# A rank-128 correction's third pass, issued as 32-row products in four banks side by side

## The chip, the cores and the metric

The kernel runs on one core of one Trainium2 chip. The metric is the device time of one execution in microseconds (us), lower being better; three runs of the kernel before are given, and one further execution was profiled.

## What is computed

The input x holds 16 batches of 512 tokens by 1024 features. A conditioning stage forms `(n*v + sum(v)) * relu(cond @ W3 + b3)`, multiplies it by `W2` (1024x1024), adds a bias and applies relu. Its result y goes through a feed-forward stage:

```
base_out   = y @ W_base + b_base                      # 1024 x 1024
shared_out = (y @ A_s) @ B_s                          # rank 16
gates      = softmax(y @ W_router + b_router), top 2 of 6 experts
routed_out = sum over e of ((y @ A_r[e]) * w_e) @ B_r[e]     # rank 16 each
out        = x + base_out + shared_out + routed_out
```

The low-rank paths of the experts and the shared one are laid side by side into one correction of rank 6 + 7*16 = 118, padded to 128 rows: `low` (128 x 1024, the B matrices) times `h` (128 x 512 tokens, gated). All products are kept accurate to about fp32 by splitting each operand into a rounded part `hi` (fp32r) and a rest `lo`, and adding three passes: hi*hi, hi*lo and lo*hi.

## The kernel before, in words

Batches are taken in pairs, eight pairs. The two large products, by `W2` (groups g = 0 to 7) and by `W_base` (g = 8 to 15, the W_base stage), are done with a seven-product scheme for 2x2 block matrices: per pair there are products n = 0 to 6, each of a 512x512 weight block by a 512x512 activation block. A product has four tiles j = 0 to 3 (128 output features each, one PSUM bank of 512 tokens each) and four steps k (128 rows of the contraction each); each step has the three passes of `three()` at L1608 to L1613. So a tile is 12 matmuls. Products 2, 3, 4 and 6 add onto a bank that already holds an earlier product (`ONTO`).

In the W_base stage the low-rank correction is added behind the twelve matmuls of each tile of products 4, 5 and 6, as three more passes over 128 rows: `low_hi` by `hi`, `low_hi` by `lo`, `low_lo` by `hi`. That makes 15 matmuls for a tile. For product 6 the operands are `ha_hi` and `ha_lo`. Product 2 is followed by four correction products of its own (`low_rank_c11`), which the change leaves alone.

The order on every engine is written out by hand and tied by semaphores. The ones that matter here:

- `bank_done` counts finished tiles on TensorE (PE), one for each tile, in program order. The VectorE (DVE) eviction `c21` of tile j of product 6 (L1142, called from `c21`) waits for its count; PE waits for `c21_done` before product 0 of the next pair overwrites the bank (`bank_free`).
- `c22_done` counts the DVE evictions of product 5; tile j of product 6 waits for the one of its bank.
- `lr_lo_done` tells that `ha_lo` (made by `lr_low_d` on DVE) is ready.
- On DVE, between the evictions of product 6, stand the operands of the next pair: the order is `low(g+1,0,0)`, `t1`, then for j = 1 to 3 `low(g+1,0,j)`, `c21(g,j-1)`, `t1(g+1,j)`. `low` (L1085) makes the `lo` part of step j of the next pair's product 0, and PE waits for it (`lo_done`) at step k of tile 0.
- The store queue (SP) writes each evicted tile to `outT` in the order of `c21_done`; at the very end the last tile is evicted and stored in two halves (L1604, L574, L1034).

Near the start `turn()` issues, between ordinary matmuls of 128 rows, four transposes of 16 rows each (L1628), of which the trace has two such groups.

Of the kernel before, what the change touches and what calls it, by code (L numbers as in the profile page):

```python
# [11 lines left out]
P = 128  # L12
# [15 lines left out]
H = 4  # L28
# [8 lines left out]

def adaln_ffn(nc, xT, condT, w3, w2, b2, wbase, bbase, acat, bcat, brouter, outT, E, R):
    NB, K, _, T = xT.shape
    NP = NB // 2  # L40
    D = K * P
# [15 lines left out]
    with ExitStack() as ctx:  # L57
        def sb(name, shape, dt=F32, stack=ctx):
            return stack.enter_context(nc.sbuf_tensor(name, shape, dt))

        def sem(name):
            return ctx.enter_context(nc.semaphore(name))
# [90 lines left out]
        low_hi = sb("low_hi", [AC, D], F32R)  # L153
        low_lo = sb("low_lo", [AC, D], F32R)
        ha_hi = sb("ha_hi", [AC, T], F32R)
# [6 lines left out]
        ps = ctx.enter_context(nc.psum_tensor("ps", [P, 8, T], F32))  # L162
# [46 lines left out]
        bank_done = sem("bank_done")  # L209
# [46 lines left out]
        lr_lo_done = sem("lr_lo_done")  # L256
        lr_done = sem("lr_done")
        c11_low = sem("c11_low")
        c11_out = sem("c11_out")
        x12_loaded = [sem(f"x12_loaded{j}") for j in range(H)]  # L260
        x22_added = sem("x22_added")
# [5 lines left out]
        def slot(g, n, k):  # L267
            return H * ((g + n) % 2) + k

        def op_no(g, n, k):  # L270
            return OPS * g + H * n + k + 1
# [8 lines left out]
        def four(g, j):  # L280
            return H * g + j + 1
# [1326 lines left out]
        def _(pe):  # L1608
            def three(out, wh, wl, a_h, a_l, start, stop, onto=False):

                nc.tensor.matmul(out, wh, a_h, start=start, stop=False, skip_group_check=onto)  # L1611
                nc.tensor.matmul(out, wh, a_l, start=False, stop=False, skip_group_check=onto)  # L1612
                return nc.tensor.matmul(out, wl, a_h, start=False, stop=stop, skip_group_check=onto)  # L1613
# [32 lines left out]
            def bank_free(g, n, j):  # L1646
                if n == 0:
                    if g > 0:
                        pe.wait_ge(c21_done, four(g - 1, j))
                elif n == 1:  # L1650
                    if g == 0:
                        pe.wait_ge(q_ready, 2)
                    elif j >= 2:
                        pe.wait_ge(c11_done, four(g, j - 2))
                    elif g == 1:
                        pe.wait_ge(c11_done, H)
                    elif g <= NP:
                        pe.wait_ge(c11_done, four(g - 1, j + 2))
                    else:
                        pe.wait_ge(c11_low, four(g - NP - 1, j + 2))  # L1660
                elif n == 2:
                    pe.wait_ge(p0_copied, four(g, j))
                elif n == 3:
                    pe.wait_ge(u2_copied, four(g, j))
                elif n == 4:
                    pe.wait_ge(u4_copied, four(g, j))
                elif n == 5:
                    pe.wait_ge(c12_done, four(g, j))
                else:
                    pe.wait_ge(c22_done, four(g, j))  # L1670

            def group(g, n, j, low_rank=None):
                bank_free(g, n, j)
                bank = j if n != 1 else Z_BANK + j % 2
                cols = slice(j * P, (j + 1) * P)
                for k in range(H):
                    if j == 0:
                        pe.wait_ge(lo_done, op_no(g, n, k))
                        if g == 0:
                            pe.wait_ge(w2_lo_done, H * n + k + 1)  # L1680
                        elif g == NP:
                            pe.wait_ge(wb_lo_done, wb_no(n, k))
                    s = slot(g, n, k)
                    mm = three(ps[:, bank, :], w_hi[:, n, k, cols], w_lo[:, n, k, cols], act_hi[:, s, :],
                               act_lo[:, s, :], k == 0 and n not in ONTO, k == H - 1 and low_rank is None, n in ONTO)
                    if j == H - 1 and k < H - 1:
                        mm.then_inc(op_used, 1)
                if low_rank is not None:
                    f, count, hi, lo = low_rank
                    if j == 0:  # L1690
                        pe.wait_ge(lr_lo_done, count)
                    cols = slice((H * f + j) * P, (H * f + j + 1) * P)
                    mm = three(ps[:, bank, :], low_hi[:, cols], low_lo[:, cols], hi[:, :], lo[:, :], False, True,
                               n in ONTO)
                mm.then_inc(bank_done, 1)
# [37 lines left out]
            def pair(i):  # L1733
                if i == 0:
                    for n in range(3):
                        first_groups(n)
                else:
                    for j in range(H):
                        group(i, 0, j)
                        project_y(i - 1, C21, j)  # L1740
                    for j in range(H):
                        group(i, 1, j)
                    for j in range(H):
                        group(i, 2, j)
                for j in range(H):
                    group(i, 3, j)
                tiles = [(c, j) for c in (C11, C12, C22) for j in range(H)]

                late = int(i == 0)
                for n in (4, 5, 6):  # L1750
                    for j in range(H):
                        group(i, n, j)
                        at = H * (n - 4) + j - late
                        if at >= 0:
                            project_y(i, *tiles[at])
                if late:
                    project_y(i, *tiles[-1])
# [80 lines left out]
```

## Time and profile before

| | us |
|---|---|
| median of 3 runs (lowest, highest) | 1411.38 (1411.37, 1411.64) |
| the profiled execution | 1411.89 |
| its span, first to last instruction | 1410.1 |
| PE busy, share of span | 1405.7, 100% |
| weight loads (PEld), share of span | 1155.8, 82% |
| DVE busy, share | 910.6, 65% |
| ScalarE (ACT) busy, share | 605.5, 43% |
| granted TensorE clock, mean | 1.000 |

The span is the profiled execution less 1.8 us around it. A matmul's record is longer than the distance to the next one, because matmuls are pipelined and their ends are modelled; the distance between starts is what a matmul costs in a row of many. A weight load has a record of its own, and may lie under the matmul before it.

### The profile page before, as it was taken

The numbers are of one execution on the slowest core, as the hardware profiler recorded it, in microseconds if no ns is written. First come the engines' busy times: TensorE is split into PE (matmuls) and PEld (weight loads), VectorE is DVE, ScalarE is ACT, GpSimd is POOL, SyncE is SP. The second block draws the span as 40 slices with busy tenths as digits, with TensorE's granted clock in tenths as the row PEclk, the third lists the DMA queues.
The fourth block names the chain that finished last, engine by engine and source line by source line (L and its number), as shares of the span: only waits on it lengthen the run. The fifth ranks groups of instructions, "written<-read, shape, count | busy, mean of one in ns | idle before, by whom it ended". The sixth has DMA issues, their size and how long they took to land.

```text
span 1410.1 us, 18033 instructions
## 1 busy us (share of the span) xinstructions
PE 1405.7 (100%) x6175; PEld 1155.8 (82%) x6175; DVE 910.6 (65%) x1563; ACT 605.5 (43%) x1136; POOL 22.1 (2%) x69
## 2 busy tenths in 40 slices
PE   9999999999999999999999999999999999999999
PEld 5888888888888888888888888888888888888887
DVE  6987565765656656567889665655655656556564
ACT  6774645546455464645544231332312323132230
POOL 3000000000000000000000000000000000000000
PEclk9999999999999999999999999999999999999999
DMA  8252414334142342426726527163361724617242
GB/s 314 67 173 82 155 54 139 106 90 155 52 141 98 104 148 59 142 83 224 266 89 208 195 95 249 61 222 136 109 239 63 246 105 136 216 60 258 94 148 91
DMA packets 135580, 200.03 MB, mean 142 GB/s; under 512 B 38752, under 2 KB 39008, under 8 KB 135488
## 3 DMA queue, kind: packets, MB, share of 16 engines
q1 hardware_dynamic: 134480, 197.39, 42.4%
q10 hardware_dynamic: 1008, 1.48, 0.3%
q8 instruction: 49, 0.80, 0.2%
q14 instruction: 43, 0.35, 0.1%
HBM read 127.12 MB, written 71.70 MB: 141 GB/s over the span
## 4 chain that ended last, share of the span: by engine, by line
PE 99%; DMA 0%; DVE 0%; DVEq 0%; issue 0%
PE ps L1611 33%; PE ps L1613 33%; PE ps L1612 33%; PE ps L1619 1%; DMA cond_b<-in_condT 0%; PE ps L1628 0%; DVE buf L1604 0%; DVEq L57 0%; PE ps L1634 0%
## 5 line engine op out<-in xcount | busy, mean ns | idle before, releaser
L1611 PE MATMUL ps<-act_hi,w_hi 128*128 128x512 f32 x1792 | 697.4, 389 | 0.0
L1612 PE MATMUL ps<-act_lo,w_hi 128*128 128x512 f32 x1792 | 697.1, 389 | 0.0
L1613 PE MATMUL ps<-act_hi,w_lo 128*128 128x512 f32 x1792 | 697.1, 389 | 0.0
L1611 PEld LDWEIGHTS ps<-act_hi,w_hi 128*128 128x128 f32 x1792 | 336.3, 188 | 70.1 <-DVE act_lo L1078 0.3
L1613 PEld LDWEIGHTS ps<-act_hi,w_lo 128*128 128x128 f32 x1792 | 336.3, 188 | 70.0
L1612 PEld LDWEIGHTS ps<-act_lo,w_hi 128*128 128x128 f32 x1792 | 336.3, 188 | 69.8
L681 ACT ACTIVATE act_hi<-src 128x512 fp32r<-128x512 f32 x256 | 156.4, 625 | 256.1 <-PE ps L1613 254.3
L1142 DVE SCALAR_TENSOR_TENSOR buf<-ps,bb_sb,buf 128x512 f32<-128x512 f32 x127 | 95.0, 749 | 157.3 <-PE ps L1613 142.3
L1085 DVE TENSOR_TENSOR act_lo<-src,act_hi 128x512 fp32r<-128x512 f32 x192 | 130.4, 684 | 36.5 <-ACT act_hi L681 36.5
L1078 DVE SCALAR_TENSOR_TENSOR act_lo<-src,shift,act_hi 128x512 fp32r<-128x512 f32 x128 | 95.2, 748 | 31.2 <-ACT act_hi L678 30.6
L700 ACT ACTIVATE yhi<-buf 128x512 fp32r<-128x512 f32 x128 | 80.0, 625 | 64.2 <-PE ps L1613 64.1
L1142 DVE SCALAR_TENSOR_TENSOR buf<-ps,b_sb,buf 128x512 f32<-128x512 f32 x92 | 68.8, 750 | 51.2 <-PE ps L1613 50.5
L1085 DVE TENSOR_TENSOR act_lo<-buf,act_hi 128x512 fp32r<-128x512 f32 x64 | 43.4, 687 | 84.6 <-ACT act_hi L681 84.5
L678 ACT ACTIVATE act_hi<-src,shift 128x512 fp32r<-128x512 f32 x124 | 87.5, 714 | 14.1 <-POOL shift L603 13.8
L708 ACT ACTIVATE buf<-ps 128x512 f32<-128x512 f32 x64 | 37.9, 597 | 120.5 <-PE ps L1613 120.5
L716 ACT ACTIVATE buf<-ps 128x512 f32<-128x512 f32 x64 | 37.9, 597 | 118.4 <-PE ps L1613 118.4
L1182 DVE TENSOR_TENSOR buf_lo<-buf,yhi 128x512 fp32r<-128x512 f32 x64 | 44.1, 688 | 55.5 <-ACT yhi L700 54.7
L727 ACT ACTIVATE buf<-ps 128x512 f32<-128x512 f32 x60 | 35.9, 598 | 84.1 <-PE ps L1613 84.1
L643 ACT ACTIVATE src<-src,qn 128x512 f32<-128x512 f32 x92 | 65.5, 712 | 0.9 <-DVE q L1047 0.9
L1082 DVE SCALAR_TENSOR_TENSOR act_lo<-src,act_hi 128x512 fp32r<-128x512 f32 x64 | 44.0, 688 | 33.2 <-ACT act_hi L681 33.1
L1611 PE MATMUL ps<-yhi,a_hi 128*128 128x512 f32 x128 | 49.8, 389 | 0.0
L1612 PE MATMUL ps<-buf_lo,a_hi 128*128 128x512 f32 x128 | 49.8, 389 | 0.0
(114 smaller groups left out, 1020.6 us busy)
## 6 DMA issues: line engine op xcount, KB each, us to landing
src<-in_xT SPq DMA_DIRECT2D x224, 256.0 KB, 2.9
y_scratch<-buf SPq DMA_DIRECT2D x128, 256.0 KB, 2.1
src<-y_scratch SPq DMA_DIRECT2D x128, 256.0 KB, 5.0
outT<-buf SPq DMA_DIRECT2D x127, 256.0 KB, 3.9
buf<-in_xT SPq DMA_DIRECT2D x32, 256.0 KB, 4.8
wl_raw<-in_wbase SPq DMA_DIRECT2D x6, 1024.0 KB, 5.9
r<-in_w SPq DMA_DIRECT2D x15, 256.0 KB, 9.6
grow<-gates_scratch SPq DMA_DIRECT2D x96, 32.0 KB, 2.1
```

What stands on the lines that cost most here:

```text
L643: nc.scalar.activation(src[:, t, :], src[:, t, :], ACT.Identity, scale=qn[:, H * HALF_OF[q] + k, 2 * i + BATCH_OF[q]:2 * i + BATCH_OF[q] + 1],
L678: nc.scalar.activation(act_hi[:, slot(g, n, k), :], source[:, t, :], ACT.Identity, bias=shift[:, t:t + 1]).then_inc(hi_done, 1)
L681: nc.scalar.activation(act_hi[:, slot(g, n, k), :], source[:, t, :], func).then_inc(hi_done, 1)
L700: nc.scalar.activation(yhi[:, (y_no(i, c, j) - 1) % 2, :], buf[:, j, :], func).then_inc(yhi_done, 1)
L1078: nc.vector.scalar_tensor_tensor(act_lo[:, s, :], source, shift[:, t:t + 1], act_hi[:, s, :].bitcast(F32), ALU.add, ALU.subtract).then_inc ...
L1082: nc.vector.scalar_tensor_tensor(act_lo[:, s, :], source, 0.0, act_hi[:, s, :].bitcast(F32), ALU.max, ALU.subtract).then_inc(lo_done, 1)
L1085: nc.vector.tensor_tensor(act_lo[:, s, :], source, act_hi[:, s, :].bitcast(F32), ALU.subtract).then_inc(lo_done, 1)
L1142: nc.vector.scalar_tensor_tensor(buf, ps[:, bank, :], bias, buf, ALU.add, ALU.add).then_inc(done, 1)
L1182: nc.vector.tensor_tensor(lo, y, hi, ALU.subtract).then_inc(ylo_done, 1)
L1611: nc.tensor.matmul(out, wh, a_h, start=start, stop=False, skip_group_check=onto)
L1612: nc.tensor.matmul(out, wh, a_l, start=False, stop=False, skip_group_check=onto)
L1613: return nc.tensor.matmul(out, wl, a_h, start=False, stop=stop, skip_group_check=onto)
```

## The change

In product 6 of the W_base stage the third pass (`low_lo` by `ha_hi`) is no longer one matmul of 128 rows for each tile. `row_tiles(r)` issues four matmuls of 32 rows: rows 0-31 for bank r, rows 32-63 for bank r+1, and so on round the four banks. Four such rounds give each bank all four strips of rows. All four rounds are issued inside tile j = 2, one behind each of its steps k = 0 to 3. The first two passes of the correction stay behind each tile.

For this, tile 2 waits at its step 0 for `lr_lo_done` and for bank 3 to be free (`bank_free(g, 6, 3)`, in addition to tile 3's own wait), each later round waits for the round before it (`rows_done`), and `bank_done` is no longer counted behind tiles 0 and 1: the end of tile 2 counts three, that of tile 3 one.

```
+            def row_tiles(r):
+                for t in range(H):
+                    j = (t + r) % H
+                    rows = slice(t * 32, (t + 1) * 32)
+                    cols = slice((H + j) * P, (H + j + 1) * P)
+                    mm = nc.tensor.matmul(ps[:, j, :], low_lo[rows, cols], ha_hi[rows, :], start=False, stop=r == H - 1,
+                                          skip_group_check=True)
+                return mm
...
                     if j == H - 1 and k < H - 1:
                         mm.then_inc(op_used, 1)
+                    if low_rank is not None and n == 6 and j == 2:
+                        if k == 0:
+                            pe.wait_ge(lr_lo_done, low_rank[1])
+                            bank_free(g, n, H - 1)
+                        if k > 0:
+                            pe.wait_ge(rows_done, (H - 1) * (g - NP) + k)
+                        tiled = row_tiles(k)
+                        if k < H - 1:
+                            tiled.then_inc(rows_done, 1)
+                if low_rank is not None and n == 6:
+                    f, count, hi, lo = low_rank
+                    if j == 0:
+                        pe.wait_ge(lr_lo_done, count)
+                    cols = slice((H * f + j) * P, (H * f + j + 1) * P)
+                    nc.tensor.matmul(ps[:, bank, :], low_hi[:, cols], hi[:, :], start=False, stop=False,
+                                     skip_group_check=True)
+                    mm = nc.tensor.matmul(ps[:, bank, :], low_hi[:, cols], lo[:, :], start=False, stop=True,
+                                          skip_group_check=True)
+
+                    if j == 2:
+                        mm.then_inc(bank_done, 3)
+                    elif j > 2:
+                        mm.then_inc(bank_done, 1)
+                    return
```

## Rows read from the trace of the kernel before

**Rows 1.** The page's head, busy time and share of the span, instructions.

```profile
span 1410.1 us, 18033 instructions
PE 1405.7 (100%) x6175; PEld 1155.8 (82%) x6175; DVE 910.6 (65%) x1563; ACT 605.5 (43%) x1136; POOL 22.1 (2%) x69
```

**Rows 2.** The page's chain that ended last, shares by engine and by line.

```profile
PE 99%; DMA 0%; DVE 0%; DVEq 0%; issue 0%
```

**Rows 3.** Waits of PE, whole span: us in total, times, longest.

```profile
PE ps L1634 <- DVE zeros L1240: 1.2, 1, 1.2
```

**Rows 4.** Groups by line and form: count, busy us, mean ns.

```profile
L1613 PE MATMUL ps<-ha_hi,low_lo 128*128 128x512 f32 x64 | 24.9, 389 | 0.0
L1613 PEld LDWEIGHTS ps<-ha_hi,low_lo 128*128 128x128 f32 x64 | 12.0, 188 | 2.5
```

**Rows 5.** Timeline of PE, product 6 of pair 5: start us, us, what.

```profile
1229.35 0.39 PE L1611 MATMUL ps<-act_hi,w_hi 128*128 128x512 f32 x1
...
1232.75 0.39 PE L1611 MATMUL ps<-act_hi,w_hi 128*128 128x512 f32 x1
...
1235.02 0.39 PE L1612 MATMUL ps<-act_lo,w_hi 128*128 128x512 f32 x1
```

**Rows 6.** Timeline of PE around four transposes of 16 rows.

```profile
16.01 0.39 PE L1613 MATMUL ps<-act_hi,w_lo 128*128 128x512 f32 x1
16.33 0.42 PE L1628 MATMUL ps<-ident,qrow 16*128 16x16 f32 x4
16.67 0.50 PE L1611 MATMUL ps<-act_hi,w_hi 128*128 128x512 f32 x1
17.01 0.40 PE L1612 MATMUL ps<-act_lo,w_hi 128*128 128x512 f32 x1
```

**Rows 7.** Timeline of the weight loads there.

```profile
16.32 0.32 PEld L1628 LDWEIGHTS ps<-ident,qrow 16*128 16x128 f32 x4 [0.35 <-issue]
16.67 0.19 PEld L1611 LDWEIGHTS ps<-act_hi,w_hi 128*128 128x128 f32 x1
16.78 0.19 PEld L1612 LDWEIGHTS ps<-act_lo,w_hi 128*128 128x128 f32 x1
```

**Rows 8.** The transposes of L1628 alone: durations in ns, min/median/max.

```profile
L1628 PE MATMUL ps<-ident,qrow x8: 201/208/231, 10.0 to 16.5; 16*128 16x16 f32 x8
```

**Rows 9.** Timeline of DVE, product 6 of pair 5.

```profile
1219.45 0.75 DVE L1142 SCALAR_TENSOR_TENSOR buf<-ps,bb_sb,buf 128x512 f32<-128x512 f32 x1 [2.65 <-PE ps L1613]
...
1221.32 0.68 DVE L1085 TENSOR_TENSOR act_lo<-src,act_hi 128x512 fp32r<-128x512 f32 x1
1222.82 0.75 DVE L1142 SCALAR_TENSOR_TENSOR buf<-ps,bb_sb,buf 128x512 f32<-128x512 f32 x1 [0.82 <-PE ps L1613]
1223.49 0.68 DVE L1101 TENSOR_TENSOR src<-src 128x512 f32<-128x512 f32 x1
1224.09 0.68 DVE L1085 TENSOR_TENSOR act_lo<-src,act_hi 128x512 fp32r<-128x512 f32 x1
1226.22 0.75 DVE L1142 SCALAR_TENSOR_TENSOR buf<-ps,bb_sb,buf 128x512 f32<-128x512 f32 x1 [1.45 <-PE ps L1613]
```

**Rows 10.** Timeline of the end, all engines.

```profile
1403.70 0.75 DVE L1142 SCALAR_TENSOR_TENSOR buf<-ps,bb_sb,buf 128x512 f32<-128x512 f32 x1 [2.65 <-PE ps L1613]
...
1406.61 0.39 PE L1613 MATMUL ps<-ha_hi,low_lo 128*128 128x512 f32 x1
1407.03 0.88 DVE L1604 SCALAR_TENSOR_TENSOR buf<-ps,bb_sb,buf 128x256 f32<-128x256 f32 x2 [2.58 <-PE ps L1613]
1407.54 0.33 SPq L574 DMA_DIRECT2D outT<-buf  x1
1407.94 0.35 ACTq L1034 DMA_DIRECT2D outT<-buf  x1
```

**Rows 11.** The page's DMA issues: KB each, median us to landing.

```profile
outT<-buf SPq DMA_DIRECT2D x127, 256.0 KB, 3.9
```

More of the change, by code:

```diff
@@ L258, in adaln_ffn @@
         c11_low = sem("c11_low")
+        rows_done = sem("rows_done")
         c11_out = sem("c11_out")
```

## The prediction, made before the changed kernel was run

> **What bounds the kernel now.** I read the page's head first: PE is busy for 1405.7 of a span of 1410.1 us, DVE for 65%, ACT for 43% [rows 1]. The chain of waits says the same from the other end: 99% of it is PE [rows 2]. PE's own waits in the whole span come to one, 1.2 us long, before the first matmul [rows 3]. So PE never waits for anyone behind its first microseconds, and whatever is added to or taken from its stream is added to or taken from the time, one for one, until something else becomes late. The price of one matmul in the stream is the distance between starts, not its record of 389 ns: a tile with correction is 15 matmuls and goes from 1229.35 to 1232.75, 3.40 us, so 0.227 us each [rows 5]. Its weight load of 188 ns [rows 4] lies under the matmul before it. The granted clock is the full one, 2.4 GHz, over the span.
>
> **What is removed.** The third pass over `low_lo` has 64 matmuls in the trace [rows 4]; half of them are product 2's corrections, and 32 (8 pairs by 4 tiles) go: 32 x 0.227 = 7.3 us.
>
> **What is added: the count.** 8 pairs by 4 rounds by 4 matmuls are 128 matmuls of 32 rows, in 32 rounds. A matmul is paid by the 512 columns that it streams, not by its rows, so four of them beside each other can at best take the slot of one, and there are as many rounds as there were matmuls: 32 slots for 32 slots. Even if the array does all that it is asked to, nothing is gained on PE; the arithmetic of the whole 128 rows was already in one matmul. What decides is what a round costs beyond one slot.
>
> **What is added: leaving and entering the 128-row stream.** The trace has one place where products over few rows stand amid ordinary matmuls at full pace: the four transposes of 16 rows at 16.33 [rows 6, 7]. Read by starts: from the last 128-row matmul (16.01) to the first transpose 0.32 us, 0.09 more than a slot. Their weight load doesn't begin under the matmul before it, as the others do, but 0.31 us after that one's start: for small strips the load isn't taken ahead. The four together last 0.42 us at 208 ns each [rows 6, 8], so the last starts 0.21 after the first, at 16.54, a pace of 0.07. The next 128-row matmul starts at 16.67, 0.13 after the last transpose. Its own load isn't hidden either: the second load follows at 16.78, 0.11 behind the first, and the second matmul at 17.01 is 0.34 later and not 0.227.
>
> A round of the change has the same shape, except that each of its matmuls streams 512 columns and not 16. At 2.4 GHz the 496 further columns are 0.207 us, and if the four run beside each other that is paid once: the step from the last start of the round to the next 128-row matmul is 0.13 + 0.207 = 0.34. With a pace p between the four starts, from the 128-row matmul ahead of a round to the second one behind it:
>
> 0.32 + 3p + 0.34 + 0.34 = 1.00 + 3p us.
>
> Before, those two slots and the removed matmul's were 3 x 0.227 = 0.68. A round therefore costs 0.32 + 3p us more than what it replaces.
>
> For p the trace gives two rows, neither of this very kind. The transposes give 0.07 (fp32, 128 columns of weights, all four on the same strip of rows) [rows 6]. The loads of fp32r weights with 128 columns give 0.11 where nothing hides them, from 16.67 to 16.78 [rows 7]. Below both stands a pace near 0, if four different strips take their weights at once; above them stands no overlap at all, p = 0.227, and if each load were bare as well 0.34. I take 0.11, the row of the same data type and width: the four loads then go one after another and the matmuls overlap in what is left. That is 0.32 + 0.33 = 0.65 us for a round, and 32 x 0.65 = 20.8 us. With 0.07 it is 0.53 and 17.0 us; with 0, 0.32 and 10.2 us; with 0.227, 1.00 and 32 us; with 0.34, 1.34 and 43 us.
>
> Two rules of the Trainium skill bear on this. "TensorEngine Tiling (Array Packing)", Key Properties, says that changing the tiling mode, not just the tile, drains the engine; this speaks against the change, since it makes 64 such switches, and the trace agrees with 0.32 and 0.34 where a slot is 0.227. "TensorE: Matmul & The Clock Gate", Part 3, gives a speedup of 3.07 for four strips of 32 rows with 512 columns; by that figure alone, without the switches, an estimate of a round is 4 x 0.227 / 3.07 = 0.30 us, 0.07 over a slot, and 32 of them 2.2 us. No row of this trace shows strips in different rows at once.
>
> **The waits that are added.** (1) `lr_lo_done` and bank 3 at step 0 of tile 2. Product 5's last eviction starts at 1219.45 and is over by 1220.2; tile 2 starts 3.40 before tile 3's 1229.35, at 1225.95, and the new wait stands behind its third matmul, 1226.6: 6.4 us of cover, and `lr_lo_done` was already waited for at tile 0's end [rows 5, 9]. Nothing. (2) `rows_done`, 24 times. The round waited for lies behind three 128-row matmuls that are ahead of the waiting one, 0.7 us or more; a DVE eviction starts 0.42 us after the start of the matmul that releases it (1406.61 to 1407.03) [rows 10], so the signal is there first. I take nothing; queued behind the wait are the round's own matmuls only. If it were exposed it is at most a bare weight load of 0.11 each, 24 x 0.11 = 2.6 us. Less than nothing is excluded for both, as a wait takes no work away. (3) `ha_lo`'s wait at tile 0 stays.
>
> **The evictions that are moved.** Tiles 0 and 1 used to be released 6.8 and 3.4 us before tile 2; now all three are released at the end of tile 2. Let T be the start of tile 3; an eviction begins 0.27 behind such a start (1226.22 against 1225.95) [rows 5, 9]. DVE has stopped at `c21` of tile 0, and behind it in its queue stand t1, low 2, `c21` 1, t1, low 3, `c21` 2, t1. By the starts of the DVE rows an eviction takes 0.67 and the others 0.60, and a low lasts 0.68 [rows 9]. Low 2 is over at T + 0.27 + 0.67 + 0.60 + 0.68 = T + 2.2, low 3 at T + 0.27 + 2 x 0.67 + 3 x 0.60 + 0.68 = T + 4.1. PE comes to product 0 of the next pair after tile 3, now 14 matmuls, at T + 3.2. Its wait for step 3 stands before the tenth matmul, 9 x 0.227 = 2.0 behind the product's start (the eleventh, the first to read that `lo`, started at 1235.02, the product at 1232.75) [rows 5], so at T + 5.2. That leaves 1.1 us; step 2's wait at T + 4.5 leaves 2.3. Banks: tile 0 of product 0 needs the eviction that is over at T + 1.0, tile 1 starts at T + 5.9 and needs one that is over at T + 2.9, the rest have more. So the move costs nothing while the cover holds; were it gone, each pair but the last would pay the excess. ACT's operands for product 0 wait for product 5 alone and are early. SP's queue waits for the fourth eviction as before, and only then goes on to the loads of the next pair; its three stores are bunched, nothing else is late.
>
> **The end of the kernel.** In the last pair the three evictions run back to back behind T (2.1 us, less than tile 3's 3.2), so the last eviction isn't late. Their stores of 256 KB, 3.9 us to landing [rows 11], start some 2 us ahead of the last two halves, where the nearest one started about 3.1 us ahead (the eviction at 1403.70 and 0.75, against 1407.54) [rows 10]. If they share the transfer engines with these, the end is 0 to 1 us later. I take 0: the stores overlapped before as well.
>
> **The sum.** On the profiled execution: 1411.9 + 20.8 = 1432.7 us, its span 1430.9. The median of the runs is 0.5 us below the profiled one, so 1411.4 + 20.8 = 1432.2 us.
>
> **The rivals.** (a) Not side by side: the 32-row matmuls take their slots one after another, each shutting out the next, so that the change doesn't do what it says. A round is then 1.00 to 1.34 us over what it replaces, 32 to 43 us in all, 1443 to 1454 us. For it: no row here shows two strips at once, and in the transposes nothing tells overlap from a short stream. Against it: they are on different strips and different banks.
> (b) Loads at once: the four strips take weights together, p near 0, and only the two switches are paid: 10.2 us, 1421.6 us. For it: the load is of separate rows. Against: both rows of a load show a pace of its own.
> (c) The other side, not slower: a round of strips is taken like any matmul, its loads ahead, under the 128-row matmul before it, and the next load under the round. Then a round costs one slot, 32 for 32, and the time is 1411.4 us; with the 0.07 of the page's speedup it is 1413.6. The point from which it decides is 2.8 / 32 = 0.09 us over a slot for each round, which would need both steps 0.32 and 0.34 of rows 6 to be the transposes' own doing and not the strips'. For it: the transposes are another operation, of another type. Against: the bare load of 0.11 in rows 7 is that of the ordinary matmul behind them.
> (d) The bunched evictions outlast their 1.1 us: it decides when DVE's 3.8 us behind T grow to 4.9, by 0.3 of themselves; grown by half, to 5.7, PE would wait 0.8 us in each of 7 pairs, 5.6 us on top of the forecast, 1438 us. Against it: all the durations of that queue are in the rows, and none of them depends on the change.
>
> **How the numbers follow.** Forecast (p between 0.07 and 0.11, and some tenths of a us either way in a switch) 50%, own range 1426 to 1437; (a) 19%; (b) 18%; (c) 8%; (d) 5%. The range of 8 in 10 takes in (b) with what may be a little cheaper than 0.32, and most of (a): 1419 to 1449. A difference under 0.2%, 2.8 us, can't be told from none here. Only (c) gives less than that: 6% within 0.2%, 2% faster, which no term of the sum gives; slower 92%.
>
> **What would show it.** The page should have 6175 - 32 + 128 = 6271 matmuls, with a group of 32-row matmuls, 128 of them, and L1613's `low_lo` group halved to 32. The timeline of one round should show the load of the first strip starting about 0.3 us after the last 128-row matmul, four starts 0.11 apart, then about 0.34 to the next 128-row matmul and 0.34 again. Tile 2 of product 6 should last 14 x 0.227 = 3.2 us plus four rounds of 0.227 + 0.65 = 0.88, 6.7 us in all, against 3.4; every other tile of the stage as before, product 6's others a slot shorter. PE should show no wait for DVE at product 0. The forecast is wrong if starts in a round are a full slot apart (a), or together (b), if a round takes 0.3 us or less (c), or if PE waits behind product 6 (d).

## The result: 13.5 us slower, 0.42 us for every round

| | before | after |
|---|---|---|
| median of the runs, us | 1411.51 (1411.37 to 1411.96) | 1425.01 (1424.41 to 1425.51) |
| ratio, 95% interval | | 1.0095 (1.0077 to 1.0112) |
| the profiled execution, its span, us | 1411.89, 1410.1 | 1424.70, 1422.9 |
| granted TensorE clock, mean | 1.000 | 1.000 |

The change is slower by 13.5 us, where 20.8 were forecast. The direction was right, and so were the cause (going in and out of the 32-row products) and the place. The pace between the starts inside a round was not, and with it the size.

The page of the changed kernel has the counts that were expected: 6271 matmuls, and a PE that is still busy throughout [rows 1].

```profile
span 1422.9 us, 18233 instructions
PE 1418.2 (100%) x6271; PEld 1153.3 (81%) x6271; DVE 907.8 (64%) x1563; ACT 605.4 (43%) x1136; POOL 21.8 (2%) x69
```

PE's waits answer to [rows 3]: two, both in the first 5 us, none behind the added waits or the moved evictions.

```profile
PE ps L1635 <- DVE zeros L1241: 1.2, 1, 1.2
PE ps L1620 <- DMA cond_b<-in_condT: 0.5, 1, 0.5
```

The groups by line and form (count, busy us, mean ns, idle before) answer to [rows 4]. `low_lo` by `ha_hi` is now 32 matmuls of 128 rows (product 2's) and 128 of 32 rows. The record of a 32-row matmul has a mean of 495 ns and not 389: it is 0.106 us longer, although it streams the same 512 columns. And its loads stand bare, that is with no matmul's stream to cover them, 32 times, where a load in the 128-row stream is hidden.

```profile
L1680 PE MATMUL ps<-ha_hi,low_lo 32*128 32x512 f32 x128 | 16.2, 495 | 0.0
L1614 PE MATMUL ps<-ha_hi,low_lo 128*128 128x512 f32 x32 | 12.4, 389 | 0.0
L1680 PEld LDWEIGHTS ps<-ha_hi,low_lo 32*128 32x128 f32 x128 | 6.1, 181 | 11.6 <-issue 11.6
```

The timeline of PE shows one round and its neighbours, in tile 2 of product 6 of pair 5 (start us, us, what). It is to be read by starts, as [rows 6]: 1233.67 to 1233.99 is 0.32, 1233.99 to 1234.43 is 0.44, 1234.43 to 1234.77 is 0.34. Together 1.10, where three slots were 0.68: 0.42 us for the round. Its four matmuls last 0.51 together at 0.496 each, so their starts are some 0.005 apart: they start at once. The whole tile lasts 5.76 us (1233.22 to 1238.98), where the prediction had 6.7.

```profile
1233.22 0.39 PE L1612 MATMUL ps<-act_hi,w_hi 128*128 128x512 f32 x1
...
1233.67 0.39 PE L1614 MATMUL ps<-act_hi,w_lo 128*128 128x512 f32 x1
1233.99 0.51 PE L1680 MATMUL ps<-ha_hi,low_lo 32*128 32x512 f32 x4
1234.43 0.50 PE L1612 MATMUL ps<-act_hi,w_hi 128*128 128x512 f32 x1
1234.77 0.39 PE L1613 MATMUL ps<-act_lo,w_hi 128*128 128x512 f32 x1
1234.99 0.40 PE L1614 MATMUL ps<-act_hi,w_lo 128*128 128x512 f32 x1
1235.32 0.51 PE L1680 MATMUL ps<-ha_hi,low_lo 32*128 32x512 f32 x4
...
1238.98 0.39 PE L1612 MATMUL ps<-act_hi,w_hi 128*128 128x512 f32 x1
```

32 rounds by 0.42 are 13.4 us, against 13.5 measured. The weight loads of the same stretch (as [rows 7]) show where it goes: nothing is loaded under the matmul ahead of a strip, or under the strips for the matmul behind them. Only the second 128-row load, at 1234.54, comes early again.

```profile
1233.45 0.19 PEld L1614 LDWEIGHTS ps<-act_hi,w_lo 128*128 128x128 f32 x1
1233.99 0.19 PEld L1680 LDWEIGHTS ps<-ha_hi,low_lo 32*128 32x128 f32 x4 [0.35 <-issue]
1234.43 0.19 PEld L1612 LDWEIGHTS ps<-act_hi,w_hi 128*128 128x128 f32 x1 [0.25 <-issue]
1234.54 0.19 PEld L1613 LDWEIGHTS ps<-act_lo,w_hi 128*128 128x128 f32 x1
```

The two bare loads, of about 0.11 us each, are half of the 0.42. The other half lies ahead of them: the strips' load starts 0.32 after the last 128-row matmul and not 0.227 (0.09), and the next 128-row load starts 0.44 after the strips, where their load and a slot would be 0.33 (0.11). What fills this half no run takes apart.

### The profile page after: what moved, and what is told of

It reads as the page before. It is cut to its first block, busy times and chain, and to the rows that moved or that the text cites. A ratio compares the mean times of both kernels' runs of the same rounds, so it can differ in the third digit from the quotient of the medians.

```text
span 1422.9 us, 18233 instructions
## 1 busy us (share of the span) xinstructions
PE 1418.2 (100%) x6271; PEld 1153.3 (81%) x6271; DVE 907.8 (64%) x1563; ACT 605.4 (43%) x1136; POOL 21.8 (2%) x69
## 4 chain that ended last, share of the span: by engine, by line
PE 99%; DMA 0%; DVE 0%; DVEq 0%; issue 0%
PE ps L1612 32%; PE ps L1614 32%; PE ps L1613 32%; PE ps L1680 1%; PE ps L1714 1%; PE ps L1620 1%; PE ps L1716 1%; DMA cond_b<-in_condT 0%; PE ps L1629 0%; DVE buf L1605 0%; DVEq L57 0%; PE ps L1635 0%
## 5 line engine op out<-in xcount | busy, mean ns | idle before, releaser
L1614 PE MATMUL ps<-yhi,a_lo 128*128 128x512 f32 x128 | 49.8, 389 | 0.0
```

## The experiments

The theory after the result, called the switch theory below: a stretch of strips amid 128-row matmuls costs 0.42 us for going in and out, whatever it holds, and each stream in it a slot. A switch here is the way in and the way out together, so the change makes 32; the prediction counted the two apart, 64. The rivals: the added waits and the bunched evictions; a price for each 32-row matmul; a price for each round wherever it stands; any matmul with fewer rows.

**The place without the strips.** Each round becomes one 128-row matmul.

```
-                for t in range(H):
-                    j = (t + r) % H
-                    rows = slice(t * 32, (t + 1) * 32)
-                    ... matmul(ps[:, j, :], low_lo[rows, cols], ha_hi[rows, :], ...)
+                cols = slice((H + r) * P, (H + r + 1) * P)
+                return nc.tensor.matmul(ps[:, r, :], low_lo[:, cols], ha_hi[:, :], start=False, stop=True, ...)
```

> Only the tiling is undone: each round is one matmul of 128 rows for one bank, at the same four places in tile 2, with the same waits (rows_done, bank 3, lr_lo_done) and the same late release of tiles 0 and 1. Switch theory (all of the cost is entering and leaving the 32-row products): 1411.5 us, within 1 us of before, 15 matmul slots where before had 15. Rival (the waits and the bunched evictions cost it): 1425 us, as the change. A mixture would stand between, and its share is the place's.

Measured: 1411.64 us against 1411.73 of before, ratio 0.9999 (0.999 to 1.0009). Its PE has the one wait of [rows 3] and no other. The waits, the place in tile 2 and the late release of tiles 0 and 1 cost nothing that shows, and by the interval no more than 1.4 us; the 13.5 us come with the 32-row matmuls.

**One strip in a round.** `for t in (0,)` in place of `for t in range(H)`.

> Each round issues only its first strip, rows 0 to 31, one matmul in place of four; three quarters of the third pass are left out. Switch theory: a round costs its switch and one stream of 512 columns whatever is beside it, so 1425 us as the change, at most 0.5 us less. Rival (each 32-row product costs about a quarter of the 0.42 us that a round costs over a slot, as four streams that disturb each other would): 0.42 less 3 x 0.105 for a round, 1411.5 + 32 x 0.105 = 1414.9 us.

Measured: 1424.91 us, ratio 1.0093 (1.0076 to 1.0109). A round of one costs what a round of four costs. Its timeline has the same three distances, 0.31, 0.43 and 0.34:

```profile
1234.05 0.39 PE L1614 MATMUL ps<-act_hi,w_lo 128*128 128x512 f32 x1
1234.36 0.50 PE L1680 MATMUL ps<-ha_hi,low_lo 32*128 32x512 f32 x1
1234.79 0.50 PE L1612 MATMUL ps<-act_hi,w_hi 128*128 128x512 f32 x1
1235.13 0.39 PE L1613 MATMUL ps<-act_lo,w_hi 128*128 128x512 f32 x1
```

**Strips of 64 rows.** Two of them side by side, four rounds; the third pass is whole.

```
-                for t in range(H):
-                    j = (t + r) % H
-                    rows = slice(t * 32, (t + 1) * 32)
+                for t in range(2):
+                    j = 2 * (r // 2) + (t + r) % 2
+                    rows = slice(t * 64, (t + 1) * 64)
...
-                    ... start=False, stop=r == H - 1,
+                    ... start=False, stop=r % 2 == 1,
```

> The third pass as products of 64 rows, two banks side by side, four rounds of two at the same places. Switch theory: the same number of switches, so 1425 us, within 1 us of the change. Rival (cost by the product): half of it is gone, 1411.5 + 32 x 0.21 = 1418.2 us.

Measured: 1425.54 us, ratio 1.0098 (1.0083 to 1.0113). Half as many matmuls, the same cost: the price by the product falls.

**One block, with the waits between its rounds.**

```
-                    if low_rank is not None and n == 6 and j == 2:
+                    if low_rank is not None and n == 6 and j == 2 and k == H - 1:
...
+                        for r in range(H):
+                            if r > 0:
+                                pe.wait_ge(rows_done, (H - 1) * (g - NP) + r)
+                            tiled = row_tiles(r)
+                            if r < H - 1:
+                                tiled.then_inc(rows_done, 1)
```

> All four rounds stand together behind step 3 of tile 2, with the waits between them: 8 switches in and out of the 32-row products in place of 32, but each later round now waits bare for the one before it. Switch theory: 8 x 0.42 = 3.4 us for the switches; between rounds a product's 0.50 us from start to end and some 0.05 for the signal in place of a slot of 0.227, 24 x 0.32 = 7.7 us; 1411.5 + 11.1 = 1422.6 us. Rival (the cost belongs to each round, wherever it stands): 1425 us or more. If the signal takes 0.3 us and not 0.05, 24 x 0.57 = 13.7, in all 1428.6 us: the timeline's distance between the rounds tells.

Measured: 1423.52 us, ratio 1.0084 (1.0069 to 1.0099), 0.9 more than forecast. By itself this time couldn't tell the theories apart: 24 switches are saved, and 24 bare waits take their place. The weight loads show them (start, us, what, what the engine waited for); the rounds are 0.58 apart, against a slot of 0.227 and the 0.55 expected:

```profile
1235.44 0.19 PEld L1680 LDWEIGHTS ps<-ha_hi,low_lo 32*128 32x128 f32 x4 [0.35 <-issue]
1236.02 0.19 PEld L1680 LDWEIGHTS ps<-ha_hi,low_lo 32*128 32x128 f32 x4 [0.39 <-PE ps L1680]
1236.60 0.19 PEld L1680 LDWEIGHTS ps<-ha_hi,low_lo 32*128 32x128 f32 x4 [0.39 <-PE ps L1680]
1237.18 0.19 PEld L1680 LDWEIGHTS ps<-ha_hi,low_lo 32*128 32x128 f32 x4 [0.39 <-PE ps L1680]
```

With 0.58 less a slot, 0.353, for each bare wait: 8 x (0.42 + 3 x 0.353) = 11.8 us, and 11.8 were measured.

**One block without waits.** As above, but `j = t` in place of `j = (t + r) % H`, so that no two strips ever meet in a bank, and no `rows_done`.

> All 16 matmuls of 32 rows stand together behind step 3 of tile 2, and each round sends strip t to bank t, so that no round has to wait for another (the result leaves out the other pairings of strips and banks). Switch theory in its plain form: inside the 32-row products a round follows the one before at a slot, its loads under it, and only 8 switches are paid: 8 x 0.42 = 3.4, 1415.1 us. Rival 1 (a strip's weights can't be loaded while that strip streams, so each round shows its load): rounds 0.33 apart, 8 x (0.42 + 3 x 0.107) = 5.9, 1417.6 us. Rival 2 (issue bounds: 0.07 for each of 16 matmuls as in the transposes): rounds 0.28 apart, 1416.4 us.

Measured: 1415.60 us, ratio 1.0029 (1.0018 to 1.004): 4.1 us over before, of which 8 x 0.42 are 3.4; the interval, 2.5 to 5.7 us, doesn't tell 4.1 from 3.4, nor from rival 2's 4.9. The timeline does. In it the block of 16 matmuls goes from 1230.76 to 1231.89, 1.13 us, where a single round has 0.44: three more rounds are 0.69, 0.23 each, in all eight pairs, where the rivals had 0.33 and 0.28. Inside the strips a round is an ordinary slot, with its loads hidden; both rivals fall.

```profile
1230.44 0.39 PE L1614 MATMUL ps<-act_hi,w_lo 128*128 128x512 f32 x1
1230.76 1.20 PE L1680 MATMUL ps<-ha_hi,low_lo 32*128 32x512 f32 x16
1231.89 0.50 PE L1710 MATMUL ps<-ha_hi,low_hi 128*128 128x512 f32 x1
1232.23 0.39 PE L1712 MATMUL ps<-ha_lo,low_hi 128*128 128x512 f32 x1
```

**The change's four places without waits.** Again `j = t`, and no `rows_done`.

> The four rounds at the change's places, but each sends strip t to bank t and none waits for the round before (the other pairings are left out). If the rows_done waits are covered by the three 128-row matmuls ahead of them: 1425.0 us as the change. If they uncover a weight load each: 24 x 0.11 less, 1422.4 us.

Measured: 1425.76 us, ratio 1.0102 (1.0087 to 1.0117). Nothing comes back; the three 128-row matmuls ahead of each wait cover it.

**Twice the switches, the same columns.** Each round is cut in two of 256 columns, behind the steps of tile 1 and of tile 2. Tile 1 therefore waits for banks 2 and 3 at its start, and each half round for the one before it.

```
+                    part = slice(half * T // 2, (half + 1) * T // 2)
+                    mm = nc.tensor.matmul(ps[:, j, part], low_lo[rows, cols], ha_hi[rows, part], ...)
...
-                    if low_rank is not None and n == 6 and j == 2:
+                    if low_rank is not None and n == 6 and j in (1, 2):
```

> Each round is split into two of 256 columns: the first half of the columns behind the four steps of tile 1, the second behind those of tile 2. The streamed columns are the same, the switches are 64 and not 32. Switch theory: 64 x 0.42 = 26.9, 1438.5 us. Rival (the cost goes with what is streamed by the strips): 1425 us.

Measured: 1439.57 us, ratio 1.0199 (1.0184 to 1.0214), 28.1 us over before: 0.44 for each of 64 switches (0.41 to 0.47 by the interval, which holds the 0.42). Twice the switches, twice the cost. From the start of the strips to the next 128-row matmul it is 0.32 with 256 columns, against 0.44 with 512, a difference close to half a slot, 0.113:

```profile
1240.37 0.39 PE L1681 MATMUL ps<-ha_hi,low_lo 32*128 32x256 f32 x4
1240.69 0.50 PE L1612 MATMUL ps<-act_hi,w_hi 128*128 128x512 f32 x1
```

**96 rows.** The 128-row matmuls of the first experiment, over `low_lo[0:96, cols]` and `ha_hi[0:96, :]`.

> As the run with 128-row matmuls at the change's places, but each over rows 0 to 95 only (22 rows of the correction's third pass are left out). If the cost comes from the array being divided into strips: 1411.5 us, as 96 rows don't fit a strip of 32 or 64. If any matmul that doesn't use all rows pays it: 1425 us.

Measured: 1412.66 us, ratio 1.0007 (0.9998 to 1.0017). It isn't the 13.5 us of the strips. The interval leaves open whether the 1.2 us of the medians are real; the timeline shows that the 96-row matmuls make no switch. The starts around them are 0.23 to 0.24 apart, with no bare load:

```profile
1226.46 0.40 PE L1677 MATMUL ps<-ha_hi,low_lo 96*128 96x512 f32 x1
1226.69 0.40 PE L1612 MATMUL ps<-act_hi,w_hi 128*128 128x512 f32 x1
1226.93 0.40 PE L1613 MATMUL ps<-act_lo,w_hi 128*128 128x512 f32 x1
1227.16 0.39 PE L1614 MATMUL ps<-act_hi,w_lo 128*128 128x512 f32 x1
1227.40 0.40 PE L1677 MATMUL ps<-ha_hi,low_lo 96*128 96x512 f32 x1
...
1229.26 0.40 PE L1677 MATMUL ps<-ha_hi,low_lo 96*128 96x512 f32 x1
```

From the first to the fourth of them it is 2.80 us, against 2.72 in the first experiment (1225.33 to 1228.05 there), and so in all eight pairs: 0.027 us a round, an estimate of 0.9 us for 32. What makes it is not shown.

**Four times the same strip.** `rows = slice(0, 32)` for all four.

> The four matmuls of each round all read rows 0 to 31 and so use the same strip of the array, for the four banks in turn (rows 32 to 127 of the third pass are left out). If the change's four really stream at once because they stand in different strips, these can't: each takes a slot of 0.227, their loads under one another, and the time is the change's 1425.0 and 32 x 3 x 0.227 = 21.8 more, 1446.8 us. Rival (32-row matmuls are cheap in themselves, in any strip): 1425 us.

Measured: 1458.24 us (1450.26 to 1462.96), ratio 1.0341 (1.032 to 1.0362), more than either the switch theory or its rival said, and with a spread that no other kernel here had. The profiled execution (1450.26, span 1448.5) shows two things. Four matmuls in one strip follow each other: 1.13 us from their start to the next 128-row matmul, against 0.44, so 0.23 more for each of three.

```profile
1247.99 1.20 PE L1680 MATMUL ps<-ha_hi,low_lo 32*128 32x512 f32 x4
1249.12 0.50 PE L1612 MATMUL ps<-act_hi,w_hi 128*128 128x512 f32 x1
```

32 x 0.69 = 22.1 on top of the change's 1425.0 would be 1447.1. The other 3 us of this execution are the clock. The table by stretches of the same product (us, busy us and count of PE, PEld, DVE, ACT and POOL, granted clock, DMA share, GB/s) has it at 1.00, then 0.87, 0.50 and back:

```profile
1248.00:1252.00 4.00, 4.00 (x15) 2.28 (x14) 0.00 (x0) 0.00 (x0) 0.00 (x0) 1.00 0.00 0
1252.00:1254.00 2.00, 2.00 (x8) 1.29 (x7) 0.00 (x0) 0.00 (x0) 0.00 (x0) 0.87 0.00 0
1254.00:1256.00 2.00, 2.00 (x5) 1.15 (x4) 0.00 (x0) 0.00 (x0) 0.00 (x0) 0.50 0.00 0
1256.00:1258.00 2.00, 2.00 (x5) 1.16 (x4) 0.11 (x1) 0.00 (x0) 0.00 (x0) 0.50 0.00 0
1258.00:1260.00 2.00, 2.00 (x6) 1.61 (x5) 2.00 (x4) 0.63 (x1) 0.00 (x0) 0.50 0.25 94
1260.00:1262.00 2.00, 2.00 (x9) 1.59 (x9) 2.00 (x4) 0.64 (x1) 0.00 (x0) 0.93 0.41 157
```

Against the full clock the stretches lack 0.13 x 2, 0.5 x 6 and 0.07 x 2, together 3.4 us of full clock, so for 6.8 us it was at 1.2 GHz in place of 2.4: 1447.1 + 3.4 = 1450.5, where 1450.3 was measured. The four executions have a mean clock of 0.997, 0.993, 0.990 and 0.988, in the order of their times: of their spans that is 4, 10, 15 and 17 to 18 us lacking, and they are 3, 9, 13 and 16 us over 1447.1. So the spread is nearly all the clock's.

## Why the prediction was right in its direction and too high

Point by point, as the prediction put it. The two steps that had the wrong size are the pace and the way out.

**The count** (nothing to gain, 32 slots for 32) held: four strips take one stream, as the starts 0.005 apart and the same-strip run show, and a round within a block is a slot of 0.23, the price of one 128-row matmul.

**Going in, 0.32, and the matmul behind, 0.34**, both read from the four transposes, are in the trace of the changed kernel to a hundredth: 0.32 and 0.34.

**The pace p = 0.11 is the step that failed.** The four loads don't follow each other. The 0.11 of [rows 7] is the time of a bare load, and I took it for a time that each strip adds; it is paid once for the round, the strips taking their weights together (four loads of 0.181 last 0.19 together). Nor could the transposes' 0.07 stand for the pace: they all used one strip of rows, and the same-strip run shows that such matmuls queue, as different strips don't. In the sum 3p was 0.33 and measured 0.015: 32 x 0.315 = 10.1 us too much.

**The way out, 0.34, was too small.** From the last start of a round to the next 128-row matmul it measured 0.425 (0.44 from the first start): 32 x 0.085 = 2.7 us too little. The prediction had 0.13 from the last transpose and 0.207 for the further columns. In the transposes the bare load came ahead of the first one, before that last start (a reading of their rows, not a test); here all four strips load bare together and start with it, as their record shows, 0.495 against 0.389. An estimate from these rows, 0.106 + 0.207 + 0.13 = 0.44, is what was measured from the first start.

The two errors make 7.4 us, against the 7.3 between 20.8 and 13.5. That they had opposite signs was luck: with the pace alone put right, the forecast would have been 10.7 us, too low by 2.8.

So of the rivals (b), loads at once, was the mechanism, and its 1421.6 us lacks the strips' bare load: with it, 32 x 0.42 = 13.4. It was given 18%, and the forecast 50%. The forecast's own range, 1426 to 1437, missed by 1 us; the full one held. Rival (a) is excluded by the timeline, by the one-strip run and by the same-strip run; (c) by each of the 32 switches.

**The waits at nothing**: right, by the run without `rows_done` and by the one with 128-row matmuls behind the same waits. Their cover was what made it so; in the block, where it is gone, each costs 0.35 us over a slot. So the prediction's "at most a bare weight load of 0.11 each" for an exposed wait was too low: at the block's price, an estimate, 24 of them would have been 8.5 us and not 2.6.

**The evictions, 1.1 us of cover**: right, and (d) with them falls. The timeline of DVE (as [rows 9]) has them bunched behind tile 2, whose successor starts at 1238.98:

```profile
1239.25 0.75 DVE L1143 SCALAR_TENSOR_TENSOR buf<-ps,bb_sb,buf 128x512 f32<-128x512 f32 x1 [9.53 <-PE ps L1716]
1239.92 0.68 DVE L1102 TENSOR_TENSOR src<-src 128x512 f32<-128x512 f32 x1
1240.52 0.69 DVE L1086 TENSOR_TENSOR act_lo<-src,act_hi 128x512 fp32r<-128x512 f32 x1
...
1242.38 0.68 DVE L1086 TENSOR_TENSOR act_lo<-src,act_hi 128x512 fp32r<-128x512 f32 x1
```

Step 3's operand is over at 1243.06. PE's tenth matmul of the next product, whose wait it is, starts at 1244.21: 1.15 us.

```profile
1242.17 0.39 PE L1612 MATMUL ps<-act_hi,w_hi 128*128 128x512 f32 x1
...
1244.21 0.39 PE L1612 MATMUL ps<-act_hi,w_hi 128*128 128x512 f32 x1
```

**The end**: right. The last matmul starts at 1419.42 in a span of 1422.9, 3.5 us before its end, as before (1406.61 of 1410.1) [rows 10].

No version with strips beat the kernel before. The cheapest, the block without waits, leaves out part of the pass and is still 4.1 us over it; the correction has 118 useful rows in one matmul of 128. That strips could save slots if several short contractions shared one is argued, not shown.

## What to carry to other kernels

Cutting a full 128-row matmul into strips gives the same number of slots. Four short products side by side would save some, by an estimate from these runs: 0.227 + 0.42 = 0.65 us for one round amid 128-row matmuls, against 4 x 0.227 = 0.91; no run here tries it.

Going from 128-row matmuls to strips and back cost 0.42 us each time here, nearly two slots of 512 columns, whether the stretch held one strip, four, or sixteen matmuls. If strips are used, put them in one stretch. A round in it that waits for the one before it costs 0.58 us and not 0.23; the block without waits avoided this by giving each strip a bank of its own, and left out part of the sum for it. Whether a whole pass can be had in one block without the waits was not tried.

And a bare load read from a trace is paid once or many times over, depending on what may load at once; a row of another operation, on one strip, doesn't tell which.

## What the runs showed of the hardware that was not expected

- Four strips load their weights and start within 0.015 us of each other; the price of a round is the same with one strip of 32 rows (1424.9 us), two of 64 (1425.5) and four of 32 (1425.0).
- Within strips loads are hidden as usual (rounds 0.23 apart). It is the passage between 128-row and strip matmuls, in both directions, that leaves a load bare, 0.11 us each, and adds as much again ahead of the loads, 0.42 in all. Matmuls of 96 rows amid those of 128 make no such passage (0.23 to 0.24 between starts).
- Rounds that use a single strip four times in a row, starting at 1247.99, 1250.01 and 1252.05, were followed by a granted clock of 0.50 (1.2 GHz) for 6.8 us in one of the eight products 6 of the profiled execution, with PE busy throughout by its records. With four strips side by side, or one strip once a round, the mean clock was 1.000. Why it fell there and not in the other seven is open.
